# A 352/288 split of an expert's rows in place of 384/256, with the third output tile computed on either side of TensorE's branch

## The reference, cut to what matters

```
logits = xn @ Wr.T                        # 8 experts
top_p, top_i = top_k(softmax(logits), 2)  # 4096 slots in all
cap = 640                                 # rows of one expert's buffer
buf[e, rank] = xn[token]                  # rank < 640 kept, the rest dropped
g, u = buf @ W12[e]                       # 256 -> 2 * 1024
h = silu(g) * u
y = h @ W3[e]                             # 1024 -> 256
out[token] += weight * y[e, rank]
```

## Time and profile before

| | us |
|---|---|
| median of 3 runs | 529.75 |
| lowest, highest | 527.85, 530.04 |
| the profiled execution | 530.99 |
| its span, first to last instruction | 529.1 |
| TensorE busy | 484.0 (91% of the span) |
| DVE busy | 352.5 (67%) |
| ACT busy | 295.1 (56%) |
| POOL busy | 187.5 (35%) |

### The profile page before, as it was taken

One profiled execution on the slowest core, in us unless ns is written; L12 is line 12 of the kernel. 1 busy time (PEld: TensorE's weight loads), 2 busy tenths in 40 slices (PEclk: granted clock), 3 DMA queues, 4 the chain that ended last, 5 costly groups with the idle time before them and its releaser, 6 DMA issues.

```text
span 529.1 us, 10749 instructions
## 1 busy us (share of the span) xinstructions
PE 484.0 (91%) x3616; PEld 447.9 (85%) x3616; DVE 352.5 (67%) x864; ACT 295.1 (56%) x744; POOL 187.5 (35%) x257
## 2 busy tenths in 40 slices
PE   5799999999999886399699999999999999999991
PEld 4677888888878764399699999999999999999991
DVE  4767879888897997648567674485843767534340
ACT  5668787687778772437365654464633747323130
POOL 7506554766867476500302121203032030311202
PEclk9899999999999997589999999999999999999997
DMA  8948422314133511172846562346451464201111
GB/s 270 277 81 244 81 31 58 74 61 103 49 74 76 195 53 59 56 259 79 258 104 209 117 203 25 72 158 164 154 114 20 131 190 133 30 8 15 14 18 20
DMA packets 41651, 57.35 MB, mean 108 GB/s; under 512 B 3721, under 2 KB 38576, under 8 KB 39552
## 3 DMA queue, kind: packets, MB, share of 16 engines
q1 hardware_dynamic: 35168, 48.62, 31.6%
q0 software_dynamic: 6144, 8.07, 9.0%
q10 hardware_dynamic: 288, 0.00, 0.0%
HBM read 36.24 MB, written 16.72 MB: 100 GB/s over the span
## 4 chain that ended last, share of the span: by engine, by line
PE 53%; issue 2%; DMA 1%; DVE 1%; POOL 1%; ACT 1%; DVEq 0%; POOLq 0%
PE bank L1468 17%; PE bank L1470 17%; PE bank L1469 17%; PE bank L1462 1%; DMA stage<-in_w3T 1%; PE bank L1389 1%; POOL expert_rows L473 1%; ACT wh L711 0%; DVE wl L1116 0%; DMA expert_rows<-xr,slotu 0%; POOL out_tokens L543 0%; PE bank L1279 0%; DVE ysc L1166 0%; PE bank L1264 0%; ACT hH L726 0%
## 5 line engine op out<-in xcount | busy, mean ns | idle before, releaser
L543 POOL DMA_INDIRECT out_tokens<-ysc,rows x32 | 49.4, 1545 | 249.1 <-DVE ysc L1166 241.9
L1468 PE MATMUL bank<-bXh,wh 128*128 128x384 f32 (+1 forms) x384 | 122.8, 320 | 4.6 <-issue 4.3
L1470 PE MATMUL bank<-bXh,wl 128*128 128x384 f32 (+1 forms) x384 | 122.4, 319 | 0.0
L1469 PE MATMUL bank<-bXl,wh 128*128 128x384 f32 (+1 forms) x384 | 122.3, 319 | 0.0
L746 ACT ACTIVATE sil<-bank 128x384 f32<-128x384 f32 (+1 forms) x96 | 43.8, 456 | 131.1 <-PE bank L1470 131.0
L1145 DVE TENSOR_TENSOR hF<-sil,bank 128x384 f32<-128x384 f32 (+1 forms) x96 | 49.0, 510 | 80.7 <-ACT sil L746 76.3
L627 ACT ACTIVATE p<-bank,nm 128x128 f32<-128x128 f32 x256 | 73.5, 382 | 25.3 <-DVE nm L926 25.3
L1468 PEld LDWEIGHTS bank<-bXh,wh 128*128 128x128 f32 x384 | 73.2, 191 | 5.0 <-issue 5.0
L1468 PE MATMUL bank<-wh,hH 128*128 128x256 f32 x256 | 73.8, 288 | 0.3 <-DVE ysc L1166 0.3
L1469 PEld LDWEIGHTS bank<-bXl,wh 128*128 128x128 f32 x384 | 73.2, 191 | 0.0
L1470 PEld LDWEIGHTS bank<-bXh,wl 128*128 128x128 f32 x384 | 73.1, 190 | 0.0
(11 more groups left out here) (144 smaller groups left out, 833.6 us busy)
## 6 DMA issues: line engine op xcount, KB each, us to landing
stage<-in_w12T SPq DMA_DIRECT2D x16, 1024.0 KB
stage<-in_w3T SPq DMA_DIRECT2D x8, 1024.0 KB
expert_rows<-padrow SPq DMA_DIRECT2D x8, 662.5 KB, 7.6
rows<-expert_rows SPq DMA_DIRECT2D x7, 662.5 KB, 4.3
kM<-k SPq DMA_DIRECT2D x64, 64.0 KB, 2.4
cT<-in_ctxT SPq DMA_DIRECT2D x8, 256.0 KB, 3.1
out_tokens<-x_all SPq DMA_DIRECT2D x8, 256.0 KB
x_all<-in_x SPq DMA_DIRECT2D x2, 640.0 KB, 8.2
```

Of the source, the lines that this page charges most:

```text
L543: pool.indirect_dma_start(out=out, out_offset=bass.IndirectOffsetOnAxis(rows[par][:, c, D + E:ROW].bitcast(U32), 0), in_=ysc[par][:, c, :] ...
L1468: nc.tensor.matmul(out_ap, ah, bh, start=start, stop=False)
L1469: nc.tensor.matmul(out_ap, ah, bl, start=False, stop=False)
L1470: return nc.tensor.matmul(out_ap, al, bh, start=False, stop=stop)
```

## The change

The first chunk gets 352 rows and the second 288. The rows of an expert are still transposed and split in pieces of 384 and 256 columns (`TILED`), so that only `up`, the hidden activations and `down` see the new widths. Output tile 2 (rows 256 to 383) now has 96 rows in chunk 0 and 32 in chunk 1. Its product is moved behind TensorE's branch: in the branch taken it is computed whole, after `up` of chunk 1, with tiles 3 and 4; in a new `Else` it is computed with the 96 rows that are there. The weighing on DVE is moved alike. `hH` and `hL` become one tensor each, since tile 2 reads across both chunks. For an expert without a second chunk the 32 last rows of tile 2 in `ysc` are never written, so POOL clears them once in both buffers, after the scatter; a new semaphore `spare_ok` tells DVE.

```diff
-CHUNKS = ((0, 384), (384, 256))
+CHUNKS = ((0, 352), (352, 288))
+TILED = ((0, 384), (384, 256))
-CT0 = CHUNKS[0][1] // P
+CT0 = 3
+SPLIT = 2
+REST = CHUNKS[0][1] - SPLIT * P
@@ tensors
-        hH = [sb(pc, f"hH{c}", [P, FT, w], F32R) for c, (_, w) in enumerate(CHUNKS)]
-        hL = [sb(pc, f"hL{c}", [P, FT, w], F32R) for c, (_, w) in enumerate(CHUNKS)]
+        hH = sb(pc, "hH", [P, FT, CAP], F32R)
+        hL = sb(pc, "hL", [P, FT, CAP], F32R)
@@ POOL, after the scatter
+            for done in scattered:
+                pool.wait_ge(done, 16 * K * SEQS // 2)
+            pool.wait_ge(pool_sent, 1)
+            pool.memset(ysc[0][REST:P, SPLIT, :], 0.0).then_inc(spare_ok, 1)
+            pool.wait_ge(spare_ok, 1)
+            pool.memset(ysc[1][REST:P, SPLIT, :], 0.0).then_inc(spare_ok, 1)
+            pool.wait_ge(spare_ok, 2)
@@ DVE
-            def weigh(e, par, t, first):
+            def weigh(e, par, t, first, n=P):
...
+                if t == SPLIT and isinstance(e, int) and e < 2:
+                    dve.wait_ge(spare_ok, e + 1)
...
-                weigh(e, par, 2, first)
                 with dve.If(more_rows(flags, e)):
                     steps(i, par, 1, last, first)
-                    for t in range(CT0, CT):
+                    for t in range(SPLIT, CT):
                         weigh(e, par, t, first)
                 with dve.Else():
+                    weigh(e, par, SPLIT, first, REST)
@@ TensorE
-            def down(e, par, c, t, parts):
-
-                o = t * P - CHUNKS[c][0]
+            def down(e, par, c, t, parts, n=P):
+
+                o = t * P
                 for f in parts:
-                    if t in (0, CT0):
+                    if t == c * SPLIT:
                         pe.wait_ge(dve_hl, 16 * e + FT * c + f + 1)
-                    ins = three(Yb[(par + t) % 2][:, 0:D],
-                                ((hH[c][:, f, o:o + P], hL[c][:, f, o:o + P]),
+                    ins = three(Yb[(par + t) % 2][0:n, 0:D],
+                                ((hH[:, f, o:o + n], hL[:, f, o:o + n]),
                                  (Wh[par][:, DC, f * D:(f + 1) * D], Wl[par][:, DC, f * D:(f + 1) * D])), f == 0, f == FT - 1)
...
-                output_bank(e, 2, first)
-                down(e, par, 0, 2, range(FT))
                 with pe.If(more_rows(flags, e)):
                     up(i, par, 1, first)
-                    for t in range(CT0, CT):
+                    for t in range(SPLIT, CT):
                         output_bank(e, t, first)
                         down(e, par, 1, t, range(FT))
+                with pe.Else():
+                    output_bank(e, SPLIT, first)
+                    down(e, par, 0, SPLIT, range(FT), REST)
```

More of the change, by code:

```diff
@@ L199, in gated_block @@
         pe_out, dve_ysc = sem("pe_out"), sem("dve_ysc")
+        spare_ok = sem("spare_ok")
         added, added2, expert_added = sem("added"), sem("added2"), sem("expert_added")
@@ L325, in _ @@
                 sp.wait_ge(scattered[s], 16 * K * SEQS // 2)
-            for (o, w), done in zip(CHUNKS, (ld_rows[0], ld_rows_rest)):
+            for (o, w), done in zip(TILED, (ld_rows[0], ld_rows_rest)):
                 if o > 0:
@@ L716, in rows_high @@
                 c, d = a // 2, a % 2
-                o, w = CHUNKS[c]
+                o, w = TILED[c]
                 act.wait_ge(pe_bT, 4 * e + a + 1)
@@ L723, in hidden_high @@
                 c, f = j // FT, j % FT
-                w = CHUNKS[c][1]
+                o, w = CHUNKS[c]
                 act.wait_ge(dve_h, 16 * e + j + 1)
-                act.activation(hH[c][:, f, :], hF[j % 2][:, 0:w], ACT.Copy).then_inc(act_hh, 1)
+                act.activation(hH[:, f, o:o + w], hF[j % 2][:, 0:w], ACT.Copy).then_inc(act_hh, 1)
             act.activation(first_silu[:, :], ident32[:, 0:1], ACT.Silu)
@@ L1148, in steps @@
                         dve.wait_ge(act_hh, 16 * e + jj + 1)
-                        dve.tensor_tensor(hL[c][:, f - 1, :], hF[jj % 2][:, 0:w], hH[c][:, f - 1, :].bitcast(F32), ALU.subtract)\
+                        dve.tensor_tensor(hL[:, f - 1, o:o + w], hF[jj % 2][:, 0:w], hH[:, f - 1, o:o + w].bitcast(F32), ALU.subtract)\
                            .then_inc(dve_hl, 1)
@@ L1159, in steps @@
                         low(i + par, 1 - par, f)
-            def weigh(e, par, t, first):
+            def weigh(e, par, t, first, n=P):
                 if t == 0 and not (isinstance(e, int) and e < 2):
                     dve.wait_ge(expert_added, e - 1)
+                if t == SPLIT and isinstance(e, int) and e < 2:
+                    dve.wait_ge(spare_ok, e + 1)
                 dve.wait_ge(pe_out, CT * e + t + 1)
-                dve.tensor_scalar(ysc[par][:, t, :], Yb[(par + t) % 2][:, 0:D], rows[par][:, t, bass.ds(D + e, 1)], None, ALU.mult)\
+                dve.tensor_scalar(ysc[par][0:n, t, :], Yb[(par + t) % 2][0:n, 0:D], rows[par][0:n, t, bass.ds(D + e, 1)], None, ALU.mult)\
                    .then_inc(dve_ysc, 1)
```

## The result

The changed kernel took 532.47 us in the median of 20 runs, the kernel before 529.9 us in 20 runs beside them: a ratio of 1.0042 with a 95% interval of 1.0027 to 1.0056. It is slower by 0.4%, where 526.7 us and a gain were forecast.

A forecast was written before the change was run, and what follows sets the result against it. TensorE, busy 91% of the span, was taken as the bound. -3.84 (experts 1, 3, 5) + 0.3 (expert 0) - 0.3 (expert 7) + 0.3 (branches) + 0.5 (expert 3's fetch) = -3.0 us, giving a median of 526.7 us; range 523.5 to 530.5.

The forecast's parts named there:

- `up` gains 1.28 us in experts 0, 1, 3, 5, nothing in the others: TensorE's `up`: 96 products each 13.3 ns shorter at 352 columns; with a second chunk, 1.28 us saved and paid back.
- The 96-row tile costs nothing: Tile 2's 24 products with 96 stationary columns: weight load hidden behind a 120 ns product as before, 0 us.
- Rival C: Tile 2's 96-column weight load stands open: 4 x 1.75 = 7.0 us on top, 533.7 us; chance 0.03.
- Expert 0's stall stays and loses its cover, +0.3 us against before: Expert 0's branch: 6.33 us code fetch stays, tile 2 no longer covers it; +0.3 us and not -1.28 us.
- Experts 1 and 3: only the branch's 0.3 us: TensorE's branch with only 0.5 us of transposes queued: 0 to 0.3 us at seven places, +0.3 us together.
- Expert 3: +0.5 us for a block just asked for: Expert 3's branch: target in the next block, just asked for under weight loads; 0 to 6.3 us, taken as +0.5.
- Rival A: Expert 3's branch waits for code, then half clock: 7.4 us in place of 0.5, 533.6 us; chance 0.12.
- Expert 7, -0.3 us: Expert 7's tile 2: its 0.29 us wait for tile 0's weighing goes, as `up` of chunk 1 stands between.
- rival D: In `up`, TensorE waits for DVE or weights, or 352 columns cost as 384; around 530 us; chance 0.11.
- POOL's clears: Two clears of 32 rows where POOL then waits 33.35 us; nothing else queued behind them, no cost.
- the jumps at the end of the branch taken: Four jumps on TensorE, covered by tile 4's queued products, no cost.
- The three shares 0.53, 0.36 and 0.11: Chances of a time below 527.1 us, within 0.5% (2.6 us) of no change, or above that.

The follow-up runs named there:

- move_only: The changed kernel with the old widths 384 and 256 and all its other edits; 537.11 us, ratio 1.0145 to the kernel before.
- first profile: Profiled execution among the changed kernel's first 20 runs, nothing edited; 529.55 us, span 527.7 us, second fastest of the 20.
- second profile: The changed kernel run and profiled once more, no edit; that execution took 532.77 us, median 531.85 us, ratio 1.0033 to the kernel before.
- before_bad: The kernel before with jumped-over instructions in `up` of expert 1 and the loop's odd expert, for a bad layout; 535.62 us, ratio 1.0128.
- all_fixed: The changed kernel with jumped-over instructions in `up` of expert 0, expert 1 and the loop's odd expert; 520.72 us, ratio 0.9827 to the kernel before.
- e1_fixed: The changed kernel with jumped-over instructions in `up` of expert 1 and the loop's odd expert, expert 0 left; 528.03 us, ratio 0.9965 to before.
- earlier_targets: As all_fixed, with other numbers of jumped-over instructions so that targets lie further from their block's end; 520.12 us, ratio 0.9803 to the kernel before.

## Why the prediction was wrong

- *`up` gains 1.28 us in experts 0, 1, 3, 5, nothing in the others.* Right. Products start 0.16 us apart at 352 columns and 0.13 at 288 (first two lines, then the last two), and the experiments put the split at 5.3 to 5.9 us (move_only), against a sum of 5.1. Two products of each width in the changed kernel:

```profile
361.41 0.32 PE L1482 MATMUL bank<-bXl,wh 128*128 128x352 f32 x1
361.57 0.32 PE L1483 MATMUL bank<-bXh,wl 128*128 128x352 f32 x1
```

```profile
317.95 0.29 PE L1482 MATMUL bank<-bXl,wh 128*128 128x288 f32 x1
318.08 0.29 PE L1483 MATMUL bank<-bXh,wl 128*128 128x288 f32 x1
```

- *The 96-row tile costs nothing.* Right in the sum; it is a little cheaper, see below. Rival C is out.
- *Expert 0's stall stays and loses its cover, +0.3 us against before.* Right in the mechanism: the branch starts at 253.2 (forecast 253.1), takes 6.32 us (6.33) and its idle time is 6.0 us. The first product of expert 1 stands 1.67 us later than before, where 0.3 was said, as half clock now falls on expert 0's tile 2 and no longer on expert 1; the two together are as forecast in the first profile. In the second profile half clock lasts longer: 1.1 us more, which nothing in the one profile of before could tell.
- *Experts 1 and 3: only the branch's 0.3 us.* This is the step that failed, for expert 1. I asked of each branch whether its target's block was there. It was (0.34 us). I didn't ask when the block behind the target would be asked for. The numbers stood in my own count: target 4,837, next block within 30 instructions, tile 2 behind it with 48. Idle time 3.3 us, for which the sum had nothing, and in part of the runs half clock behind it. Forecast and measured median lie 5.8 us apart: this idle time is 3.3 of them, and experts 0 to 2 take 3.3 us more in the second profile, nearly all of it half clock. Before, the same branch's target was 85 instructions ahead of the block's end, nearly all of them in `up`, and tile 2 was queued in front.
- *Expert 3: +0.5 us for a block just asked for.* Not there (0.47 us for the branch, TensorE busy all through; the block had landed at 355.19 us, the branch starts at 357.7), though before_bad shows that this stall exists.
- *Rival A: a second branch waits for code, slower by 0.7%, 533.6 us.* That is nearly what came (532.5), at another place and by a neighbouring mechanism: straight code behind the branch ran out, and not the branch. It had 0.12; that its time fits is luck, as neither its branch nor its 7.4 us came.
- *Expert 7, -0.3 us.* It gained 0.56 us: 0.29 of waiting, and 0.27 that I haven't traced. All of it is from the move: move_only has it with the old widths. *DVE as the next bound (rival D), POOL's clears, the jumps at the end of the branch taken:* nothing of them shows.
- *What would show it.* Of the three signs of being wrong (another branch of over 1 us, no long branch at expert 0, idle time ahead of a product of `up`) none came: the stop stands in tile 2, where I had named no sign.
- *The three shares 0.53, 0.36 and 0.11.* They don't follow from the chances: A and C, both above, have 0.15.

In short: the split gives 5.3 to 5.9 us; moving tile 2 behind the branch takes 7.6 with the layout that this program happens to get, by the fetch of code at experts 0 and 1. With another layout the same code gives 1.7 to 2.0% against the kernel before; 0.7% of that is the stall of the kernel before, which a shift takes away there as well, and 1.0 to 1.3% is the change.

## What to carry to other kernels

A branch on TensorE is not only its own duration: look at where its target lies in the blocks of the program, at how many instructions are left there, and at what work is queued ahead of the branch. Work behind a branch covers nothing; tile 2 ahead of it covered 2 us of the 6.3 us fetch at expert 0. And when any edit changes the number of instructions ahead of a far branch, some microseconds can come or go that have nothing to do with the edit; a few skipped instructions tell them apart.

## What the runs showed of the hardware

- A branch to a block that wasn't asked for takes 3.8 us with small weight loads (DMA engines 23 to 33% busy), and 5.9 to 6.9 us under weight loads of 1 MB. In every profile here, at each stop of 0.44 us and more in the experts, TensorE goes on 1.2 to 1.7 us after a 16 KB packet of its instruction queue has landed (before_bad's expert 3: its branch ends 1.4 us after).
- The idle time of straight code behind a target falls with the distance to its block's end, where nothing is queued ahead of the branch: 3.3 to 3.5 us where it runs out after 29 instructions, 0.45 to 0.59 us with 74 to 86 instructions by the count (all_fixed, e1_fixed), none over 0.3 us with 96 and 101 (earlier_targets).
- Blocks once used stay, as far as this loop goes: in its second pass in the changed kernel (1,460 instructions) no branch of TensorE takes over 0.25 us, and no instruction packet of its queue moves from 362.1 to 431.6 us.
- A float32r product with 96 stationary columns starts 0.116 us after the one before it (ten steps from 286.47 to 287.63 in the changed kernel), with 128 it is 0.119 (290.19 to 291.38 in move_only). Why the three nanoseconds are saved isn't shown. The Trainium skill ("TensorE: Matmul & The Clock Gate", section "Weight-path perf modes") ties the fast weight load to 128 weights of a type that isn't float32; nothing was lost here with 96; whether the products with 128 have the fast load isn't shown by any run.
- In the same program the idle time of expert 1 is followed by full clock in one execution (3.34 us idle, then 1.00) and by half clock in another (3.54 us idle, then 0.54).
